# Turning the normed input of a gated-attention stage by DMA transposes through DRAM instead of TensorE transposes

## The chip, the cores and the metric

The kernel runs on one Trainium2 chip, on 8 cores. Every core runs the same program on its own stretch of 4096 tokens (plus 128 tokens of warm-up ahead of it), with its own copy of the weights; the cores exchange nothing. The time is that of the slowest core, in microseconds. The engines are called as in the profile: PE (TensorE, matrix products), PEld (its weight loads), DVE (VectorE), ACT (ScalarE), POOL (GpSimd) and SP (SyncE, which issues all DMAs here).

## The reference

One layer of gated linear attention, and one channel-mixing layer behind it, both in a residual frame with LayerNorms. The input is two sequences of 16384 tokens with 1024 features, in float32.

```python
def _L0_attn_ref(x, Wq, Wk, Wv, Wo, norm_w):
    q = silu(x @ Wq.T);  f = sigmoid(x @ Wk.T);  log_f = log_sigmoid(f)
    k = 1.0 - f;         v = x @ Wv.T
    out = _gla_scan(heads(q), heads(k), heads(v), heads(log_f))   # 8 heads of 128
    return _rmsnorm(out, norm_w) @ Wo.T
# _gla_scan, per token: S = exp(g) * S + k outer v ; o = q . S
def _L0_ffn_ref(x, W_r, W_k, W_v, mu_r, mu_k):
    xr = mu_r * x + (1 - mu_r) * x_prev;  xk = mu_k * x + (1 - mu_k) * x_prev
    return sigmoid(xr @ W_r.T) * (square(relu(xk @ W_k.T)) @ W_v.T)
x = x + layernorm(_L0_attn_ref(layernorm(x), ...))
x = x + layernorm(_L0_ffn_ref(layernorm(x), ...))
```

## The kernel before, in words

**Numbers in pairs.** Every float32 operand of a matrix product is held as two bf16 tensors, a high part (`_h`) and a low part (`_l`), and every product is three bf16 products added in PSUM: high by high, high by low, low by high.

**Tiles.** A tile `p` is 256 tokens (tile 0 has the 128 of warm-up alone), in two chunks `j` of 128. There are `nt` = 17 tiles, 0 to 16. Stage A computes q, k, v and the attention, and writes its output to the DRAM tensors `oh_scr` and `ol_scr`. Stage B reads it back, applies Wo and the first residual, and does the channel mixing with three more weights. Weights of stage B take the SBUF places of stage A's as these come free; between the stages lies a stretch in which both are interleaved by hand.

**One tile of stage A.** The tokens of tile p+1 are loaded as `xt` (128 tokens on the partitions, 2 chunks, 1024 features, float32). `ln_stats` finds mean and variance, `ln_apply` (line 394, ACT) norms `xt` in place. The matrix products need the features on the partitions, so `turn_x` transposes: for each chunk and each half of the features, four PE transposes of 128x128 in float32 into one PSUM bank (line 409), then ACT copies the bank to bf16 as `lnh` (line 416), and DVE subtracts that from the bank to give `lnl` (line 418). `lnh` and `lnl` each have two buffers, for even and odd tiles.

**The order of the work** is written out by hand. A helper appends each instruction to its engine's list, with semaphore waits; each engine runs its list in order. The loop over p = 2 to 15 issues, in this order: `k_tile(p)` (k of the tile, 192 products, line 251), `ln_stats(p+1)`, `gate(p)`, `gla_scores(p-1,0)` (lines 547 and 572, results split as `A_h`, `A_l`, `Ax_h`, `Ax_l`), `q_job(p,0)` and `(p,1)` (line 251), `ln_apply(p+1)`, `scan(p,0)` (line 481, DVE), `gla_out(p-1,0)` (line 607), `gla_scores(p-1,1)`, `q_job(p,2)` and `(p,3)`, `scan(p,1)`, `gla_rms(p-1,0)` (line 632), `gla_out(p-1,1)`, `turn_x(p+1)`, `load_x(p+2)`, `v_job(p,0,0)` (line 234), `gla_rms(p-1,1)`, `store_o(p-1)`, `prep(p,0)`, and the other three `v_job`s with `prep(p,1)`. Thus `turn_x` is called for tiles 3 to 16 in this loop, and for tiles 0 to 2 ahead of it. `k_tile(p+1)`, the first use of the turned tile, is the first thing PE does in the next round.

**PSUM** is a ring of 8 banks: `take()` hands out the next, and its user first waits until the bank's last reader is done. `turn_x` takes four of them for each tile.

**DMAs** are all on SP's list, in order, among them the load of `xt` (which waits until the last transpose has read the tile), and the stores of `os_h` and `os_l` to `oh_scr` and `ol_scr`. `wst` is a buffer of 8 KB on each partition in which the last two rows of blocks of each weight land; after the weights of stage A it is not used until stage B's come.

Of the kernel before, what the change touches and what calls it, by code (L numbers as in the profile page):

```python
# [9 lines left out]
ALU = mybir.AluOpType  # L10
# [82 lines left out]
def build_program(tok, warm):  # L93
# [16 lines left out]
    oh_scr = nc.dram_tensor("oh_scr", [nt * 128, NCH * TILE], BF16).ap()  # L110
    ol_scr = nc.dram_tensor("ol_scr", [nt * 128, NCH * TILE], BF16).ap()

    xNc = xN.rearrange("(n p) d -> p n d", p=128)
    outNc = outN.rearrange("(n p) d -> p n d", p=128)

    def o_dram(scr, p):
# [1 line left out]

    ctx = ExitStack()
    sets = {"wk": 0, "wq": 1, "wv": 2, "wo": 0, "wk2": 1, "wr": 2, "wv2": 0}  # L120
    bld = Bld(nc, ctx, ["LC", "LI", "LX", "LX0", "LX1", "LO0", "LO1", "SO", "SB0", "SB1",
                        "V", "S", "G", "T"] + [f"W{i}{ci}" for i in range(3) for ci in range(NCH)])
    op, ev, C = bld.op, bld.ev, bld.cnt

    def sb(stack, name, shape, dt):
        return stack.enter_context(nc.sbuf_tensor(name, shape, dt))
# [16 lines left out]
    aa = sb(ctx, "aa", [128, 6], F32)  # L143
    bb = sb(ctx, "bb", [128, 6], F32)
    rv = sb(ctx, "rv", [128, 2], F32)
    wst = sb(ctx, "wst", [128, 2, D], F32)
    ring = [ctx.enter_context(nc.psum_tensor(f"ps{i}", [128, 512], F32)) for i in range(8)]

# [184 lines left out]
    with ExitStack() as early:  # L333
        with ExitStack() as first:
# [13 lines left out]

    at = {"xt": [], "lnT": [[], []], "kf": [], "qs": [], "gb": [], "ebq": [], "ebk": [], "pl": [],
          "qt": [[], []], "kt": [[], []], "kx": [[], [], []], "vt": [[], [], []], "A": [],  # L350
          "Ax": [], "os": [], "osq": [], "rv": [[], []]}
    ck = {}

    def half_of(p):
# [45 lines left out]
    def turn_x(p, js=None, banks=None):  # L400
        for j in js or half_of(p):
            xj = x_of(p, j)
            dh, dl, js = ln_of(p, j)
            free = at["lnT"][p % 2] if p else []
            for g in range(2):
                i, bank = (banks[g], ring[banks[g]]) if banks else take()
                for b in range(4):
                    c = 4 * g + b
                    op("tensor", lambda e, b=b, c=c, xj=xj, bank=bank: e.transpose(  # L409
                        bank[:, b * 128:(b + 1) * 128], xj[:, c * 128:(c + 1) * 128],  # L410
                        ident[:]),
                       wait=[ln_ab[p, j], ev_id] + ring_free[i] if b == 0 else (),
                       inc=[("T", 1)] if b == 3 else ())
                evt = ev("T")
                b3 = bank[:].rearrange("p (c n) -> p c n", n=128)
                evh = sop(lambda e, g=g, js=js, dh=dh, b3=b3: e.activation(
                    out=dh[:, 4 * g:4 * g + 4, js], in_=b3, func=AF.Copy), evt, *free)
                evl = vop(lambda e, g=g, js=js, dh=dh, dl=dl, b3=b3: e.tensor_tensor(
                    dl[:, 4 * g:4 * g + 4, js], b3, dh[:, 4 * g:4 * g + 4, js],
                    ALU.subtract), evh)  # L420
                ring_free[i] = [evl]
        if p == 0:
            at["kf0"] = [evt]
        else:
            at["xt"] = [evt]
        ck[p] = dict(lnT=evl)

    def put_k(p, i, bank, evt, blocks):
        kp, _, _, fs = own(p)
# [44 lines left out]
    def v_job(p, j, half, *waits):  # L474
        xh, xl, js = ln_of(p, j)
        put_v(p, j, half, *tok_job(xh, xl, js, *pair("wv"), half, *waits))

    def scan(p, j):
        _, _, gp, js = own(p, j)
        for h in range(H):  # L480
            evb = op("vector", lambda e, h=h: e.tensor_tensor_scan(  # L481
                gp[:, h, js], gp[:, h, js], gp[:, h, js], 0.0, ALU.add, ALU.bypass),
                wait=[("V", C["V"]), ck[p]["g"]] if h == 0 else (), inc=[("V", 1)], nop=True)
        ck[p][f"b{j}"] = evb
# [103 lines left out]
    def gla_out(p, j):  # L588
        n = 2 * p - 1 + j
        js = slice(j * 128, (j + 1) * 128)  # L590
        c = ck[p]
        s0, s1 = n % 3, (n - 1) % 3
        for g4 in range(2):
            i, bank = take()
            parts = [(s0, ((vt_h, A_h), (vt_h, A_l), (vt_l, A_h)), [c[f"A{j}{g4}"], c[f"v{j}"]])]
            if n > 0:
                bp, bj = before(p, j)
                parts.append((s1, ((vt_h, Ax_h), (vt_h, Ax_l), (vt_l, Ax_h)),
                              [c[f"X{j}{g4}"], ck[bp][f"v{bj}"]]))
            for k, (sv, pairs, waits) in enumerate(parts):  # L600
                for m in range(12):
                    h = 4 * g4 + m // 3
                    vo, ao = pairs[m % 3]
                    cs = slice((m // 3) * 128, (m // 3 + 1) * 128)
                    first, last = k == 0 and m == 0, k == len(parts) - 1 and m == 11
                    op("tensor", lambda e, vo=vo, ao=ao, sv=sv, h=h, cs=cs, g4=g4, first=first,
                       last=last, bank=bank: e.matmul(  # L607
                           bank[:, cs], vo[:, sv, h, :], ao[:, g4, cs], start=first, stop=last),
                       wait=waits + (ring_free[i] if first else []) if m == 0 else (),
                       inc=[("T", 1)] if last else ())  # L610
            evt = ev("T")
            b3 = bank[:].rearrange("p (h n) -> p h n", n=128)
            h4 = slice(4 * g4, 4 * g4 + 4)
            evh = sop(lambda e, b3=b3, h4=h4: e.activation(
                out=os_h[:, h4, js], in_=b3, func=AF.Copy), evt, *at["os"])
            evq = sop(lambda e, g4=g4, bank=bank: e.activation(
                out=osq[:, g4 * 512:(g4 + 1) * 512], in_=bank[:], func=AF.Square), *at["osq"])
            evl = vop(lambda e, b3=b3, h4=h4: e.tensor_tensor(
                os_l[:, h4, js], b3, os_h[:, h4, js], ALU.subtract), evq)
            ring_free[i] = [evl]  # L620
        at["A"] = at["Ax"] = [evt]
        at["vt"][s1] = [evt]
        c[f"o{j}"] = evl
        c[f"sq{j}"] = evq
# [109 lines left out]
    for p in range(2, nt - 1):  # L734
        k_tile(p)
        ln_stats(p + 1)
        if p == 2:
            gla_out(0, 1)
        gate(p)
        gla_scores(p - 1, 0)  # L740
        if p == 2:
            gla_rms(0, 1)
            store_o(0)
        q_job(p, 0)
        q_job(p, 1)
        ln_apply(p + 1)
        scan(p, 0)
        gla_out(p - 1, 0)
        gla_scores(p - 1, 1)
        q_job(p, 2)  # L750
        q_job(p, 3)
        scan(p, 1)
        gla_rms(p - 1, 0)
        gla_out(p - 1, 1)
        turn_x(p + 1)
        if p + 2 < nt:
            load_x(p + 2)
        v_job(p, 0, 0)
        gla_rms(p - 1, 1)
        store_o(p - 1)  # L760
        prep(p, 0)
        v_job(p, 0, 1)
        v_job(p, 1, 0)
        prep(p, 1)
        v_job(p, 1, 1)
        bld.flush()
# [348 lines left out]
```

How the kernel before makes its waits and increments, by code:

```python
        def closure(e, fn=fn, waits=waits, incs=tuple(incs), nop=nop):  # L51
            for sem, v in waits:
                e.wait_ge(sem, v)
            if nop:
                e.engine_nop()
            ins = fn(e)
            for sem, k in incs:
                ins.then_inc(sem, k)
# [11 lines left out]
        def closure(e, waits=waits):  # L70
            for sem, v in waits:
                e.wait_ge(sem, v)
```

## Time and profile before

| what | value |
|---|---|
| time, median of 3 runs | 2744.53 us |
| the profiled execution's own time | 2742.91 us |
| its span (slowest core, core 2) | 2741.1 us |
| spans of all 8 cores | 2739.5 to 2741.1 us |
| PE busy | 2635.0 us (96%) |
| DVE busy | 1279.0 us (47%) |
| ACT busy | 1113.5 us (41%) |
| POOL busy | 409.6 us (15%) |
| DMA, mean over the span | 43 GB/s |
| mean granted clock of PE | 0.984 |

The span is the time between the first and the last instruction of a core, and lies 1.8 us under the execution's own time. Busy shares are averages over two stages and the stretch between them: the loop of stage A runs from about 150 to 1205 us, the stretch between to about 1430 us, and stage B from there to the end. The granted clock is 1.00 where the chip lets PE run at its upper level of 2.4 GHz throughout, and 0.50 where it is held at the lower, 1.2 GHz. A busy PE says that products are in its pipeline, so what an instruction costs there is read from the distance between starts, as the chain of waits and the timeline give it, and not from its duration.

### The profile page before, as it was taken

The numbers are of one execution on the slowest core, as the hardware profiler recorded it, in microseconds if no ns is written. First come the engines' busy times: TensorE is split into PE (matmuls) and PEld (weight loads), VectorE is DVE, ScalarE is ACT, GpSimd is POOL, SyncE is SP. The second block draws the span as 40 slices with busy tenths as digits, with TensorE's granted clock in tenths as the row PEclk, the third lists the DMA queues.
The fourth block names the chain that finished last, engine by engine and source line by source line (L and its number), as shares of the span: only waits on it lengthen the run. The fifth ranks groups of instructions, "written<-read, shape, count | busy, mean of one in ns | idle before, by whom it ended". The sixth has DMA issues, their size and how long they took to land.

```text
span 2741.1 us, 53464 instructions; the slowest of 8 cores (2739.5 to 2741.1 us)
## 1 busy us (share of the span) xinstructions
PE 2635.0 (96%) x19752; PEld 1783.9 (65%) x19752; DVE 1279.0 (47%) x2148; ACT 1113.5 (41%) x1349; POOL 409.6 (15%) x350
## 2 busy tenths in 40 slices
PE   6989999999999999998749999999999999999998
PEld 5778777777788877775436555665565654556544
DVE  6354444444444443435555444544445444454443
ACT  4555555555555555555343222222222222222222
POOL 0223333232222333322000000000000000000000
PEclk9999999999999999999879999999999999999999
DMA  7000010001000010024230011100111001110000
GB/s 226 17 10 31 32 32 32 32 32 32 32 33 29 5 32 32 32 62 139 78 108 22 34 39 47 46 33 24 39 47 47 32 24 39 47 47 32 24 27 28
DMA packets 39888, 118.97 MB, mean 43 GB/s; under 512 B 11728, under 2 KB 11984, under 8 KB 39632
## 3 DMA queue, kind: packets, MB, share of 16 engines
q1 hardware_dynamic: 39632, 115.56, 12.4%
q8 instruction: 160, 2.62, 0.4%
q14 instruction: 96, 0.79, 0.1%
HBM read 81.47 MB, written 34.08 MB: 42 GB/s over the span
## 4 chain that ended last, share of the span: by engine, by line
PE 88%; DVE 5%; ACT 3%; POOL 2%; issue 1%; DMA 1%; DVEq 0%; ACTq 0%; POOLq 0%; SPq 0%
PE ps L234 46%; PE ps L251 33%; PE ps L607 3%; PE ps L572 1%; PE ps L547 1%; PE ps L274 1%; PE ps L409 1%; PE ps L845 1%; DVE st L287 1%; DVE wk L213 1%; DMA wst<-wqT 1%; DVE gb L481 0%; POOL ebk L500 0%; DVE wr L213 0%; POOL kx_l L525 0%
## 5 line engine op out<-in xcount | busy, mean ns | idle before, releaser
L251 PE MATMUL ps<-xk_h,wk 128*128 128x256 bf16 x2048 | 340.4, 274 | 3.5 <-DVE wk L213 3.5
L251 PE MATMUL ps<-lnh,wq 128*128 128x256 bf16 x1920 | 322.1, 274 | 0.0
L234 PE MATMUL ps<-wo,o_h 128*128 128x512 bf16 x1056 | 314.7, 380 | 2.7 <-DVE A_l L558 2.7
L251 PE MATMUL ps<-lnh,wk 128*128 128x256 bf16 x1920 | 316.9, 273 | 0.0
L234 PE MATMUL ps<-wr,xr_h 128*128 128x512 bf16 x1024 | 306.5, 381 | 10.3 <-DVE wr L213 10.3
L234 PE MATMUL ps<-wv,lnh 128*128 128x512 bf16 x1056 | 314.1, 379 | 0.0
L234 PE MATMUL ps<-wv,kc_h 128*128 128x512 bf16 x1024 | 304.6, 379 | 0.0
L251 PE MATMUL ps<-xk_l,wk 128*128 128x256 bf16 x1024 | 280.3, 274 | 0.0
L251 PE MATMUL ps<-lnl,wq 128*128 128x256 bf16 x960 | 263.0, 274 | 0.0
L251 PE MATMUL ps<-lnl,wk 128*128 128x256 bf16 x960 | 261.7, 273 | 0.0
L292 POOL TENSOR_TENSOR aa<-v,mhalf 128x1 f32<-128x1 f32 x98 | 53.7, 548 | 1157.4 <-DVE v L290 1157.1
L251 PEld LDWEIGHTS ps<-xk_h,wk 128*128 128x128 bf16 x2048 | 201.3, 98 | 29.2 <-issue 3.6
L251 PEld LDWEIGHTS ps<-lnh,wq 128*128 128x128 bf16 x1920 | 188.8, 98 | 22.4
L251 PEld LDWEIGHTS ps<-lnh,wk 128*128 128x128 bf16 x1920 | 187.9, 98 | 23.2
L234 PE MATMUL ps<-wo,o_l 128*128 128x512 bf16 x528 | 200.4, 380 | 0.0
L234 PE MATMUL ps<-wv,lnl 128*128 128x512 bf16 x528 | 200.1, 379 | 0.0
L234 PE MATMUL ps<-wr,xr_l 128*128 128x512 bf16 x512 | 195.1, 381 | 0.0
L234 PE MATMUL ps<-wv,kc_l 128*128 128x512 bf16 x512 | 194.1, 379 | 0.0
L234 PEld LDWEIGHTS ps<-wr,xr_h 128*128 128x128 bf16 x1024 | 100.5, 98 | 132.3 <-issue 12.8
L234 PEld LDWEIGHTS ps<-wo,o_h 128*128 128x128 bf16 x1056 | 103.4, 98 | 124.2 <-issue 3.4
L234 PEld LDWEIGHTS ps<-wv,lnh 128*128 128x128 bf16 x1056 | 102.1, 98 | 117.5
L234 PEld LDWEIGHTS ps<-wv,kc_h 128*128 128x128 bf16 x1024 | 100.2, 98 | 117.5
(146 smaller groups left out, 4460.6 us busy)
## 6 DMA issues: line engine op xcount, KB each, us to landing
xt<-xN SPq DMA_DIRECT2D x16, 1024.0 KB, 8.1
x<-xN SPq DMA_DIRECT2D x16, 1024.0 KB, 5.7
outN<-x SPq DMA_DIRECT2D x32, 512.0 KB, 2.7
oh_scr<-os_h SPq DMA_DIRECT2D x16, 512.0 KB, 8.8
ol_scr<-os_l SPq DMA_DIRECT2D x16, 512.0 KB, 9.6
o_h<-oh_scr SPq DMA_DIRECT2D x15, 512.0 KB, 4.2
o_l<-ol_scr SPq DMA_DIRECT2D x15, 512.0 KB, 5.1
wk_f<-wkT SPq DMA_DIRECT2D x6, 512.0 KB, 11.8
```

Of the source, the lines that this page charges most:

```text
L213: evl = vop(lambda e, ci=ci, sl=sl: e.tensor_tensor(wl[:, ci, :], sl, wh[:, ci, :], ALU.subtract), evh)
L234: op("tensor", lambda e, xo=xo, wo=wo, ci=ci, first=first, last=last: e.matmul(bank[:], xo[:, ci, js], wo[:, ci, hs], start=first, stop=last),
L251: last=last: e.matmul(bank[:, os], wo[:, ci, ds], xo[:, ci, ts], start=first, stop=last),
L274: first=first, last=last: e.matmul(bank[:, cs], so(ci), mo(ci), start=first, stop=last),
L287: vop(lambda e, src=src, h=h: e.bn_stats(st6[:, k, 6 * h:6 * h + 6], src), *waits[h])
L292: evp = gop(lambda e: e.tensor_tensor(aa[:, k:k + 1], v1[:, k:k + 1], mhalf[:], ALU.pow), ev1, ev_set, *ab_free[k])
L409: op("tensor", lambda e, b=b, c=c, xj=xj, bank=bank: e.transpose(bank[:, b * 128:(b + 1) * 128], xj[:, c * 128:(c + 1) * 128], ident[:]), ...
L547: op("tensor", lambda e, ko=ko, qo=qo, h=h, cs=cs, m=m, bank=bank: e.matmul(bank[:, cs], ko[:, sl, h, :], qo[:, sl, h, :], start=m == 0, s ...
L572: op("tensor", lambda e, ko=ko, qo=qo, h=h, cs=cs, m=m, bank=bank: e.matmul(bank[:, cs], ko[:, sx, h, :], qo[:, sl, h, :], start=m == 0, s ...
L607: last=last, bank=bank: e.matmul(bank[:, cs], vo[:, sv, h, :], ao[:, g4, cs], start=first, stop=last),
L845: op("tensor", lambda e, b=b, c=c, bank=bank: e.transpose(bank[:, b * 128:(b + 1) * 128], lnd[:, j, c * 128:(c + 1) * 128], ident[:]), wai ...
```

## The change

Tiles 3 to 16 (the calls in the loop) no longer go through `turn_x`. In its place:

- `ln_pair(p+1)`, right behind `scan(p,0)`: for each chunk ACT copies the normed `xt` to bf16 and DVE subtracts the copy from `xt`, both 128x1024, still with the tokens on the partitions. The pair lies in a new buffer `lnp`, which has the SBUF place of `wst`.
- `turn_dma(p+1)`, behind `load_x(p+2)` on SP's list: one DMA writes `lnp` (1 MB) to a DRAM tensor `ln_scr`, and when it has landed, two DMA transposes (256x1024 in bf16, 512 KB each) read it back turned, into `lnh` and `lnl`.
- `load_x(p+2)` waits for the last subtraction of `ln_pair` instead of the last PE transpose.
- `k_tile(p+1)` waits for the second DMA transpose. The PSUM ring is asked for 26 banks in a round instead of 30.

```diff
+    ln_scr = nc.dram_tensor("ln_scr", [4 * TILE, D], BF16).ap()
...
+    with ExitStack() as raw:
+        lnp = sb(raw, "lnp", [128, 2, 2, D], BF16)
     wst = sb(ctx, "wst", [128, 2, D], F32)
...
+    def ln_pair(p):
+
+        for j in range(2):
+            evh = sop(lambda e, j=j: e.activation(out=lnp[:, 0, j, :], in_=xt[:, j, :],
+                                                  func=AF.Copy),
+                      ln_ab[p, j], *wst_free[0], *wst_free[1])
+            evl = vop(lambda e, j=j: e.tensor_tensor(lnp[:, 1, j, :], xt[:, j, :],
+                                                     lnp[:, 0, j, :], ALU.subtract), evh)
+        at["xt"] = [evl]
+
+    def turn_dma(p):
+
+        b = p % 2
+        rows = ln_scr[2 * b * TILE:(2 * b + 2) * TILE, :]
+        evs = dma(rows.rearrange("(a j p) d -> p (a j) d", a=2, p=128),
+                  lnp[:].rearrange("p a j d -> p (a j) d"), "SL", *at["xt"], *at["turned"][b])
+        wst_free[0] = wst_free[1] = [evs]
+        for a, dst in enumerate((lnh[b], lnl[b])):
+            evt = op("sync", lambda e, a=a, dst=dst: e.dma_start_transpose(
+                out=dst[:], in_=rows[a * TILE:(a + 1) * TILE, :]),
+                wait=[evs] + at["lnT"][b], inc=[("LT", 16)])
+        at["turned"][b] = [evt]
+        ck[p] = dict(lnT=evt)
...
         scan(p, 0)
+        ln_pair(p + 1)
         gla_out(p - 1, 0)
...
         gla_out(p - 1, 1)
-        turn_x(p + 1)
         if p + 2 < nt:
             load_x(p + 2)
+        turn_dma(p + 1)
         v_job(p, 0, 0)
```

The change moves line numbers by up to 30. On SP, one round of the loop before (the load of `xt`, the two stores of attention output):

```order
L159 DMA xt<-xN 128x2x1024
L159 DMA oh_scr<-os_h 128x2048
L159 DMA ol_scr<-os_l 128x2048
L87 UNCONDITIONAL_BRANCH
L159 DMA xt<-xN 128x2x1024
L159 DMA oh_scr<-os_h 128x2048
```

The same place on SP now:

```order
L163 DMA xt<-xN 128x2x1024
L163 DMA ln_scr<-lnp 128x4x1024
L451 DMA_TRANSPOSE lnh<-ln_scr 128x8x256
L451 DMA_TRANSPOSE lnl<-ln_scr 128x8x256
L163 DMA oh_scr<-os_h 128x2048
L163 DMA ol_scr<-os_l 128x2048
```

Three DMAs have come in between the load and the stores.

On ACT, from the norming of `xt` to the first `v_job`'s copy, before (`os_h` and `osq` are `gla_out`'s results, `vt_h` is v's high part):

```order
L394 ACTIVATE xt<-xt,bb,aa 128x1024 x2
L614 ACTIVATE os_h<-ps 128x4x128
L616 ACTIVATE osq<-ps 128x512
L614 ACTIVATE os_h<-ps 128x4x128
L616 ACTIVATE osq<-ps 128x512
L554 ACTIVATE A_h<-ps 128x512 x2
L578 ACTIVATE Ax_h<-ps 128x512 x2
...
L616 ACTIVATE osq<-ps 128x512
L416 ACTIVATE lnh<-ps 128x4x128 x4
L445 ACTIVATE vt_h<-ps 128x512
```

The same stretch of ACT now:

```order
L399 ACTIVATE xt<-xt,bb,aa 128x1024 x2
L436 ACTIVATE lnp<-xt 128x1024 x2
L643 ACTIVATE os_h<-ps 128x4x128
L645 ACTIVATE osq<-ps 128x512
L643 ACTIVATE os_h<-ps 128x4x128
L645 ACTIVATE osq<-ps 128x512
L583 ACTIVATE A_h<-ps 128x512 x2
L607 ACTIVATE Ax_h<-ps 128x512 x2
...
L645 ACTIVATE osq<-ps 128x512
L474 ACTIVATE vt_h<-ps 128x512
```

Four copies from PSUM behind `gla_out(p-1,1)` are gone, and two longer ones stand ahead of `gla_out(p-1,0)`'s results.

On DVE, around the scan of the first chunk (line 481 before), before, from the last of the eight scans on:

```order
L481 SCALAR_TENSOR_TENSOR gb<-gb 128x128
L618 TENSOR_TENSOR os_l<-ps,os_h 128x4x128 x2
L552 TENSOR_TENSOR ps<-ps,mask 128x512 x2
L558 TENSOR_TENSOR A_l<-ps,A_h 128x512 x2
L580 SCALAR_TENSOR_TENSOR Ax_l<-ps,Ax_h 128x512 x2
```

And now:

```order
L510 SCALAR_TENSOR_TENSOR gb<-gb 128x128
L439 TENSOR_TENSOR lnp<-xt,lnp 128x1024 x2
L647 TENSOR_TENSOR os_l<-ps,os_h 128x4x128 x2
L581 TENSOR_TENSOR ps<-ps,mask 128x512 x2
L587 TENSOR_TENSOR A_l<-ps,A_h 128x512 x2
L609 SCALAR_TENSOR_TENSOR Ax_l<-ps,Ax_h 128x512 x2
```

Two subtractions now stand ahead of the work on `gla_out(p-1,0)` and `gla_scores(p-1,1)`.

## Rows read from the trace of the kernel before

**Rows 1.** The page's first part: busy time by engine.

```profile
PE 2635.0 (96%) x19752; PEld 1783.9 (65%) x19752; DVE 1279.0 (47%) x2148; ACT 1113.5 (41%) x1349; POOL 409.6 (15%) x350
```

**Rows 2.** Chain of waits, 675.9 to 755 us: start, length, what.

```profile
675.85 20.96 PE ps L251 x192
...
725.99 2.70 PE ps L607 x48
728.69 1.75 PE ps L409 x16
730.44 5.18 PE ps L234 x24
...
751.36 3.71 PE ps L251 x34
```

**Rows 3.** Busy time by window, core 2; the columns head the group.

```profile
core 2: us, PE busy (x) PEld busy (x) DVE busy (x) ACT busy (x) POOL busy (x), PEclk, DMA share, GB/s
...
675.85:751.36 75.51, 75.51 (x706) 59.82 (x705) 32.52 (x57) 42.10 (x53) 21.48 (x16) 1.00 0.08 29
```

**Rows 4.** Line 409 in the loop, 150 to 1300 us.

```profile
L409 PE MATMUL ps<-ident,xt x224: 272/273/278, 199.9 to 1183.2; 128*128 128x128 f32 x112
```

**Rows 5.** For whom PE waited, 150 to 1300 us: total, times, longest.

```profile
PE ps L572 <- ACT kf L430: 4.3, 1, 4.3
PE ps L632 <- ACT osq L616: 3.4, 2, 3.1
```

**Rows 6.** Timeline of ACT, 706 to 737 us.

```profile
710.87 2.63 ACT L394 ACTIVATE xt<-xt,bb,aa 128x1024 f32<-128x1024 f32 x2
713.70 0.60 ACT L614 ACTIVATE os_h<-ps 128x512 bf16<-128x512 f32 x1 [0.20 <-ACT xt L394]
...
720.14 1.34 ACT L578 ACTIVATE Ax_h<-ps 128x512 bf16<-128x512 f32 x2
...
730.53 2.83 ACT L416 ACTIVATE lnh<-ps 128x512 bf16<-128x512 f32 x4
735.72 0.60 ACT L445 ACTIVATE vt_h<-ps 128x512 bf16<-128x512 f32 x1 [2.36 <-PE ps L234]
```

**Rows 7.** Timeline of DVE, 706 to 737 us.

```profile
707.23 2.84 DVE L481 TENSOR_TENSOR_SCAN gb<-gb 128x128 f32<-128x128 f32 x8 [0.20 <-DVE Ax_l L580]
715.14 0.69 DVE L618 TENSOR_TENSOR os_l<-ps,os_h 128x512 bf16<-128x512 f32 x1 [5.07 <-ACT osq L616]
...
722.02 0.69 DVE L580 SCALAR_TENSOR_TENSOR Ax_l<-ps,Ax_h 128x512 bf16<-128x512 f32 x1 [0.17 <-DVE Ax_l L580]
722.91 2.83 DVE L481 TENSOR_TENSOR_SCAN gb<-gb 128x128 f32<-128x128 f32 x8 [0.20 <-DVE Ax_l L580]
...
731.35 0.69 DVE L418 TENSOR_TENSOR lnl<-ps,lnh 128x512 bf16<-128x512 f32 x1 [0.17 <-DVE os_l L618]
```

**Rows 8.** Lines 502 and 504: durations in ns, minimum, median, maximum.

```profile
L502 ACT ACTIVATE qt_h<-ebq x33: 1057/1057/1058, 120.0 to 1282.0; 128x1024 bf16<-128x1024 f32 x33
...
L504 DVE TENSOR_TENSOR qt_l<-ebq,qt_h x33: 1225/1762/1989, 121.2 to 1283.2; 128x1024 bf16<-128x1024 f32 x33
```

**Rows 9.** Timeline of SP, 706 to 737 us: DMAs issued.

```profile
730.52 0.38 SPq L159 DMA_DIRECT2D xt<-xN  x1
731.25 0.32 SPq L159 DMA_DIRECT2D oh_scr<-os_h  x1
731.66 0.38 SPq L159 DMA_DIRECT2D ol_scr<-os_l  x1
```

**Rows 10.** DMA issues: count, KB each, us from issue to landing.

```profile
x<-xN SPq DMA_DIRECT2D x16, 1024.0 KB, 5.7
...
ol_scr<-os_l SPq DMA_DIRECT2D x16, 512.0 KB, 9.6
...
wv_f<-wvT SPq DMA_DIRECT2D x6, 512.0 KB, 18.3
...
o_h<-oh_scr SPq DMA_DIRECT2D x3, 256.0 KB, 6.7
...
oh_scr<-os_h SPq DMA_DIRECT2D x1, 256.0 KB, 3.1
```

**Rows 11.** Windows of 10 us, columns as in group 3.

```profile
150.00:160.00 10.00, 7.57 (x93) 6.91 (x91) 3.94 (x6) 4.07 (x6) 6.62 (x4) 1.00 0.01 2
160.00:170.00 10.00, 5.07 (x43) 4.25 (x44) 4.40 (x10) 8.30 (x11) 3.42 (x4) 0.51 0.00 1
170.00:180.00 10.00, 10.00 (x76) 8.24 (x75) 6.09 (x14) 6.93 (x8) 2.19 (x3) 0.81 0.27 55
```

More of the change, by code:

```diff
@@ L120, in build_program @@
     sets = {"wk": 0, "wq": 1, "wv": 2, "wo": 0, "wk2": 1, "wr": 2, "wv2": 0}
-    bld = Bld(nc, ctx, ["LC", "LI", "LX", "LX0", "LX1", "LO0", "LO1", "SO", "SB0", "SB1",
+    bld = Bld(nc, ctx, ["LC", "LI", "LX", "LX0", "LX1", "LO0", "LO1", "SO", "SL", "LT", "SB0", "SB1",
                         "V", "S", "G", "T"] + [f"W{i}{ci}" for i in range(3) for ci in range(NCH)])
@@ L350, in build_program @@
           "qt": [[], []], "kt": [[], []], "kx": [[], [], []], "vt": [[], [], []], "A": [],
-          "Ax": [], "os": [], "osq": [], "rv": [[], []]}
+          "Ax": [], "os": [], "osq": [], "rv": [[], []],
+          "turned": [[], []]}
     ck = {}
```

## The prediction

> **What bounds the kernel now.** I read the busy times first: PE is busy 96% of the span, no other engine half of it [rows 1]. That is an average, so next came the chain of waits through one round of stage A's loop [rows 2]. There the reader is to see that every piece from one `k_tile` (675.85 us) to the next (751.36 us) is PE's own, each starting where the last ended: PE is never released by anybody in these 75.51 us. The busy window says the same: 75.51 of 75.51 us, at a granted clock of 1.00, the upper level of 2.4 GHz, while DVE works 32.5 us, ACT 42.1 us and the DMA engines are 8% busy [rows 3]. In the whole loop PE waits for another engine three times, 7.7 us together, all near 160 us [rows 5, 11]. So in this stage a microsecond taken from PE is a microsecond off the time, as long as everything else stays inside the shorter round; and nothing taken from ACT or DVE is worth anything by itself.
>
> **What the change removes from PE.** The 16 transposes of a tile stand in the chain for 1.75 us, from 728.69 to 730.44 [rows 2], or 109 ns from start to start (the 273 ns of a single one is its way through the pipeline [rows 4]). Line 409 has 224 of them in the loop, at 199.9 to 1183.2 us, with no spread in their durations (272 to 278 ns), so 14 tiles at one price [rows 4]. 14 x 1.75 = **24.5 us**. The transposes of tiles 0 to 2 stay.
>
> **What it removes from ACT and DVE.** Four copies (2.83 us) and four subtractions of 0.69 us behind `gla_out(p-1,1)` [rows 6, 7]. Neither engine is waited for there: ACT idled 2.36 us before the copy of the first `v_job`, until PE had finished it [rows 6]. Worth nothing, but that copy and the `prep` chain behind it start 1.75 us earlier, as PE does, so the rear part of the round moves as a block.
>
> **What it adds to ACT and DVE, ahead of work that PE waits for.** A copy of 128x1024 to bf16 took 1.06 us and a subtraction of that shape 1.76 us (1.23 to 1.99) [rows 8]. ACT is done with norming at 713.50 us and was late already: `os_h` began 0.20 us behind it [rows 6]. Two copies with gaps put `os_h` 2.4 us later, at 716.1. On DVE the first subtraction starts when the first copy ends, about 714.9, the second ends near 718.6; DVE was idle for 5.07 us before 715.14 [rows 7], so the first hides. The subtraction for `os_l`, which started at 715.14, now starts at 718.8. Behind it stand the masks, `A_l` and `Ax_l` of `gla_scores(p-1,1)`. Their last ended at 722.71 [rows 7]; DVE loses its small gaps, ACT's `A_h` and `Ax_h` (from 720.14) move too [rows 6], and I work the last out to end near 725.5, 2.8 us later. Who waits for it: `gla_out(p-1,1)` on PE, at 725.99 [rows 2], under cover of the two `q_job`s. It needs the first `Ax_l` only behind 12 of its 48 products, and the second later still. The cover is eaten but holds: **0 us**. If it didn't hold, each microsecond late costs one per tile, 14 us in all. The second scan ends near 728.6 instead of 725.7: only `prep` reads it, which stands behind the copy of the first `v_job` (735.72 before [rows 6]). The ring: with 26 banks per round each job takes a bank used by another job 8 places earlier; the closest case is the first `v_job`, whose bank then comes from `gla_scores(p-1,1)`, free near 724 and wanted at 728.7. The 56 takes left out are seven turns of the ring, so stage B has the banks it had.
>
> **What it adds on SP and the DMA engines.** This decides the case. Data are ready at 718.6 us. SP first issues the load of `xt` (now at about 718.8 instead of 730.52), then the store of 1 MB. Before, a load of 1 MB and stores of 1 MB went out from 730.52 to 731.66 and the last landed 9.6 us behind its issue, so 2 MB took 10.7 us from first issue to last landing [rows 9, 10]. The same 2 MB now: landed by 729.5. SP stands in its wait until then. Queued behind it are the transposes and then the two stores of attention output, whose data are not ready before about 730 anyway, and whose next reader in line, the overwriting of `os_h`, comes a round later, at 713.70 plus a round [rows 6]. `k_tile(p+1)` wants the turned pair at 751.36 - 1.75 = 749.6. So the two DMA transposes, 1 MB in all, have **20.1 us**; every microsecond over that stalls PE by one in each of 14 rounds, and PE has nothing else in its list to do.
>
> No DMA transpose is in this trace, so its time D for the pair has to be bounded. Fast end: a plain load of 1 MB with nothing in its way, 5.7 us [rows 10]: 14 us to spare. Middle: pieces of 256 bytes. The first store of `os_h` goes in such pieces (128 tokens in bf16), 256 KB in 3.1 us, four of which are 12.4 us: hidden. The read of `oh_scr` in like pieces took 6.7 us for 256 KB, in other traffic, which gives 26.8 us: 6.7 us late [rows 10]. Slow end: a 512 KB load that stood in a full queue took 18.3 us, twice that is 36.6 us: 16.5 us late [rows 10]. I take the store of 256-byte pieces, 12.4 us, since the queue is nearly empty here (29 GB/s in a round [rows 3]), and so a cost of 0.
>
> The Trainium skill, page "Advanced Engine Details and Errata", section "X-Bar Transpose (TRN2)", says that transposing DMAs on this chip are as fast as plain ones, at 350 to 400 GB/s; by it the pair would take an estimated 3 us and the sum is the same. No row here shows it.
>
> **The sum.** Span 2741.1 - 24.5 = 2716.6; the execution's own time 2742.9 - 24.5 = 2718.4; the median of the runs lies 1.6 us over that execution, so **2720.0 us**, 0.9% faster. A measurement of this kernel can tell about 2% from no change, so this counts as within 2%.
>
> **Rival 1: the transposes are late, somewhat.** Place: PE in front of `k_tile(p+1)`, releaser the second transpose. Point from which it decides: D over 20.1 us; from 21.9 us on the kernel is slower than before, from 25.8 us by over 2% (55 us / 14 = 3.9 us per tile, and the 1.75 given back). With 26.8 us: 14 x (6.7 - 1.75) = +69 us, 2814 us. It can be worse: where PE idled 7.4 us between 150 and 170 us, the clock stood at 0.51 and then 0.81 for 10 us each, a loss of 10 x (0.49 + 0.19) = 6.8 us [rows 11]. If each stall does that, 14 x 11.75 = +165 us, 2909 us. For it speaks that 256-byte pieces have been that slow once; against it, that this was in a stretch with much other traffic.
>
> **Rival 2: the transposes go block by block and are far too slow.** At 36.6 us: 14 x (16.5 - 1.75) = +207 us, 2951 us, and 3047 us with the loss of clock. The extreme is a transpose that moves single elements: 262,144 for each of two parts at 3.1 us per 1024 pieces [rows 10] are 1.6 ms per tile and some 22 ms in all.
>
> The Trainium skill, page "VectorE: DVE Perf Modes", section "The three transpose paths", puts 1309 ns on one 128x128 block through the DMA path; the pair has 32 blocks, and by an estimate from that page, if they go one behind another, 42 us, 22 us late, about 3025 us. This is the rule that speaks against the change; no row here shows whether blocks overlap.
>
> **Rival 3: ACT and DVE run out of cover.** `A_l` and `Ax_l` come 1 to 2 us behind PE's need instead of 0.5 us ahead, because DVE's subtractions take their slow form and ACT falls behind. It gives back 14 to 28 us: 2734 to 2748 us. The work lies 2.8 us closer to PE than before, which speaks for it; the order of the products in `gla_out`, which asks for `Ax_l` last, against.
>
> That the change doesn't do what it says is out: the program's order has the 14 groups of transposes gone from PE.
>
> **Chances.** Forecast 0.70 (2714 to 2734 us); rival 3 0.05; rival 1 0.07; rival 2 0.17; anything that makes it faster by over 2%, 0.01. The most likely is 2720. The range must leave out no more than 2 in 10: it goes from 2712 to 2909, which has the forecast, rival 3 and rival 1 with its clock loss (0.82), and leaves rival 2 out. A part of rival 1 (D between 20.1 and 25.8 us) is still within 2%: same 0.77, slower 0.22, faster 0.01.
>
> **What would show it.** Right: in a round of the loop the chain holds PE alone and `k_tile` starts are 73.76 us apart; line 409 has 40 transposes left; the two DMA transposes land before about 750 us minus what earlier rounds saved; PE has no wait on them; `Ax_l` ends just before `gla_out`. Wrong: a wait of PE in front of `k_tile` with a DMA into `lnl` as its releaser, rounds of over 75.5 us, and a granted clock under 1.00 in them. What would make the forecast wrong is above all D, and next the landing of the store, since the store and the transposes share the same 30.8 us.

## Result and the profile after

The time of the changed kernel, in the executions that are compared, is 2719.8 us against 2744.5 us: a ratio of 0.991, 95% interval 0.9894 to 0.9927. That is 24.7 us less, on a forecast of 24.5 us. The profiled execution took 2719.81 us, with spans of 2716.4 to 2718.0 us. (Some executions of either kernel ran with one die or both at a lower granted clock and are left out of every comparison here, so a median over all of them would mislead.) A second series later gave 2718.5 to 2719.8 us for the same kernel (median 2719.3), beside 2743.1 us for the kernel before: 23.8 us less.

The busy times of the page, for the slowest core (core 0), beside [rows 1]:

```profile
PE 2601.8 (96%) x19383; PEld 1758.8 (65%) x19528; DVE 1274.3 (47%) x2120; ACT 1109.7 (41%) x1321; POOL 409.5 (15%) x350
```

The chain of waits through one round of stage A's loop, beside [rows 2] (start, length, what; where the record of a product is missing, the chain is interrupted by 0.05 us of "issue"):

```profile
664.79 20.96 PE ps L255 x192
...
714.93 2.70 PE ps L636 x48
717.63 0.05 issue
717.68 5.13 PE ps L238 x23
...
738.55 20.96 PE ps L255 x192
```

From one `k_tile` to the next are 738.55 - 664.79 = 73.76 us, where it was 75.51. The piece of 1.75 us between `gla_out` and the first `v_job` is gone, and nothing has come in its place. The window (core 0; columns as in [rows 3]) says that PE runs through, at a granted clock of 1.00, with more than twice the DMA share:

```profile
664.79:738.55 73.76, 73.60 (x688) 58.06 (x689) 32.21 (x55) 41.83 (x51) 21.48 (x16) 1.00 0.22 58
```

For whom PE waited between 150 and 1250 us, beside [rows 5]: the same two entries, and no DMA. (Up to 1300 us there is a third, 9.8 us for `lnd` near 1280, in the stretch between the stages. The kernel before has it too, with 9.4 us, behind 1300.)

```profile
PE ps L601 <- ACT kf L459: 4.3, 1, 4.3
PE ps L661 <- ACT osq L645: 3.4, 2, 3.1
```

What goes on meanwhile is on SP. Its timeline through the same round (start, time that SP needs to issue, what):

```profile
706.72 0.38 SPq L163 DMA_DIRECT2D xt<-xN  x1
707.25 0.39 SPq L163 DMA_DIRECT2D ln_scr<-lnp  x1
718.08 2.72 SPq L451 DMA_TRANSPOSE lnh<-ln_scr  x1
720.95 2.37 SPq L451 DMA_TRANSPOSE lnl<-ln_scr  x1
723.41 0.74 SPq L163 DMA_DIRECT2D oh_scr<-os_h  x1
724.25 0.38 SPq L163 DMA_DIRECT2D ol_scr<-os_l  x1
```

and from the list of DMA issues, the time from issue to landing in us:

```profile
ln_scr<-lnp SPq DMA_DIRECT2D x14, 1024.0 KB, 10.7
...
lnh<-ln_scr SPq DMA_TRANSPOSE x14, 5.8
lnl<-ln_scr SPq DMA_TRANSPOSE x14, 5.6
```

The store is issued at 707.25 and the first transpose at 718.08, when it has landed. By the median of the list, the second transpose lands 5.6 us behind 720.95, at about 726.6: the pair has taken D = 8.5 us, and `k_tile` wants it at 738.55. So 11.9 us are left over.

On DVE the timeline shows what [rows 7] showed, with the two subtractions in front:

```profile
704.02 1.23 DVE L439 TENSOR_TENSOR lnp<-xt,lnp 128x1024 bf16<-128x1024 f32 x1 [5.00 <-ACT lnp L436]
705.42 1.23 DVE L439 TENSOR_TENSOR lnp<-xt,lnp 128x1024 bf16<-128x1024 f32 x1 [0.17 <-DVE lnp L439]
706.82 0.69 DVE L647 TENSOR_TENSOR os_l<-ps,os_h 128x512 bf16<-128x512 f32 x1 [0.17 <-ACT osq L645]
...
713.64 0.69 DVE L609 SCALAR_TENSOR_TENSOR Ax_l<-ps,Ax_h 128x512 bf16<-128x512 f32 x1 [0.17 <-DVE Ax_l L609]
```

The last `Ax_l` ends at 714.33, 0.6 us before `gla_out` begins at 714.93. Before it was 722.71 against 725.99, 3.3 us [rows 2, 7]. The cover proper is larger, since `gla_out` asks for the first `Ax_l` only at its 13th product: that product starts at 715.46 by PE's timeline, and the first `Ax_l` ended at 713.47, 2.0 us earlier.

### The profile page after: what moved, and what is told of

The parts are those of the page before. It is cut to its first block, busy times and chain, and to the rows that moved or that the text cites. A ratio compares the mean times of both kernels' runs of the same rounds, so it can differ in the third digit from the quotient of the medians.

```text
span 2718.0 us, 52729 instructions; the slowest of 8 cores (2716.4 to 2718.0 us)
## 1 busy us (share of the span) xinstructions
PE 2601.8 (96%) x19383; PEld 1758.8 (65%) x19528; DVE 1274.3 (47%) x2120; ACT 1109.7 (41%) x1321; POOL 409.5 (15%) x350
## 2 busy tenths in 40 slices
DMA packets 105517, 148.30 MB, mean 55 GB/s; under 512 B 70192, under 2 KB 70448, under 8 KB 105264
## 4 chain that ended last, share of the span: by engine, by line
PE 86%; DVE 5%; ACT 3%; issue 2%; POOL 2%; DMA 1%; DVEq 0%; ACTq 0%; POOLq 0%; SPq 0%
PE ps L238 45%; PE ps L255 33%; PE ps L636 3%; PE ps L576 1%; PE ps L601 1%; PE ps L278 1%; PE ps L875 1%; DVE st L291 1%; DMA wst<-wqT 1%; DVE xm L897 1%; DVE wk L217 1%; POOL ebk L529 0%; DVE wr L217 0%; DVE gb L510 0%; DVE x L854 0%
## 5 line engine op out<-in xcount | busy, mean ns | idle before, releaser
L238 PE MATMUL ps<-wr,xr_h 128*128 128x512 bf16 x994 | 300.2, 381 | 11.2 <-DVE wr L217 10.3
L238 PE MATMUL ps<-wv,lnh 128*128 128x512 bf16 x1023 | 307.0, 379 | 2.5
L238 PE MATMUL ps<-wo,o_l 128*128 128x512 bf16 x513 | 194.8, 380 | 0.1
L238 PE MATMUL ps<-wv,lnl 128*128 128x512 bf16 x513 | 194.5, 379 | 0.1
L238 PE MATMUL ps<-wv,kc_l 128*128 128x512 bf16 x497 | 188.5, 379 | 0.1
## 6 DMA issues: line engine op xcount, KB each, us to landing
ln_scr<-lnp SPq DMA_DIRECT2D x14, 1024.0 KB, 10.7
```

The costliest lines, as they stand in the source:

```text
L238: op("tensor", lambda e, xo=xo, wo=wo, ci=ci, first=first, last=last: e.matmul(bank[:], xo[:, ci, js], wo[:, ci, hs], start=first, stop=last),
```

## Experiments

The theory to test has three parts: the gain is PE's 1.75 us per tile and nothing else; the DMA route is free as long as store and transposes fit in their room; and ACT and DVE sit inside PE's need by little. The rivals: part of the gain or of the cost lies on ACT and DVE, or in the traffic. All line numbers are those of the kernel in question.

### Nothing turned at all (e1_no_turn)

```diff
-        ln_pair(p + 1)
...
+        ck[p + 1] = dict(lnT=ln_ab[p + 1, 1])
+        at["xt"] = [ln_ab[p + 1, 1]]
         if p + 2 < nt:
             load_x(p + 2)
-        turn_dma(p + 1)
```

> Leaves out the turning of tiles 3 to 16 altogether: no copy to bf16, no subtraction, no store, no transposes; k, q and v of these tiles are worked out from what stood in the buffers. My theory: the new route costs nothing, so this takes what the changed kernel takes, 2720 us (within 2 us). Rival: the new route costs something that only a comparison shows (contention, cover eaten on ACT and DVE); then this is faster than the changed kernel by 14 times that cost, 2706 us for 1 us per tile.

Measured: 2720.1 to 2720.8 us, ratio to the kernel before 0.9918 (0.9898 to 0.9937). Without copies, subtractions, stores and transposes the kernel is no faster than with them (2718.5 to 2719.8 us). So the new route costs nothing that can be measured, and taking the turning away altogether wins no more than this change does.

### PE turns as before, the pair is made and stored besides (e2_both)

```diff
+        pair_ev = list(at["xt"])
+        turn_x(p + 1)
+        at["xt"] = at["xt"] + pair_ev
         if p + 2 < nt:
             load_x(p + 2)
-        turn_dma(p + 1)
+        store_pair(p + 1, pair_ev)      # the store of turn_dma alone
```

> PE still turns tiles 3 to 16 as in the kernel before, and the bf16 pair is made and stored to DRAM besides (no DMA transposes, nobody reads the pair). My theory: the whole gain is the 1.75 us of PE per tile, and what was added is free, so this takes what the kernel before takes, 2744.5 us (within 2 us). Rival: part of the gain came from relieving ACT and DVE behind the transposes; here they carry both loads, and it would be slower than before, by 14 us for each microsecond that PE is kept waiting in a round.

Measured: 2744.2 to 2745.1 us, ratio 1.0013 (1.0000 to 1.0026). ACT and DVE carry the old load and the new, and the time is that of the kernel before beside it (median 2743.2) to 1.7 us. With PE's transposes back the gain is gone, so the gain is PE's. The chain of waits has the transposes back at their old price:

```profile
727.65 2.70 PE ps L644 x48
730.36 1.75 PE ps L414 x16
732.11 5.18 PE ps L238 x24
```

### The transposes two, three and four times (e3_twice, e4_thrice, e4b_four)

The pair of transposes is issued again when the last one has landed, so that only D grows:

```diff
-        for a, dst in enumerate((lnh[b], lnl[b])):
-            evt = op("sync", ..., wait=[evs] + at["lnT"][b], inc=[("LT", 16)])
+        for _ in range(2):          # 3, 4
+            gate_ev = [evs] + at["lnT"][b] + ([evt] if _ else [])
+            for a, dst in enumerate((lnh[b], lnl[b])):
+                evt = op("sync", ..., wait=gate_ev, inc=[("LT", 16)])
```

> The pair of DMA transposes is done twice, the second time when the first has landed. In the trace of the changed kernel the store lands 53.3 us behind the start of k_tile, the pair takes about 8.5 us more, and the next k_tile starts at 73.76 us: 11.9 us to spare. A second pair uses 8.5 of them. My theory: still hidden, 2720 us. Rival (traffic of the transposes slows something that PE reads or waits for): slower by 14 us for each microsecond per tile.

> The pair of DMA transposes is done three times, one behind the other: 25.5 us instead of 8.5, against 20.4 us of room, so 5.1 us late per tile. My theory: PE waits in front of k_tile in 14 rounds, 2720 + 14 x 5.1 = 2791 us if a stall of that length costs only itself. Rival: each such stall also lowers the granted clock, as the 7.4 us near 160 us seem to do, and costs up to 6.8 us more: up to 2887 us, with a granted clock under 1.00 behind each stall.

> The pair of DMA transposes is done four times, one behind the other. With three, a pair took about 8.0 us there and PE waited 1.7 us per tile. My theory: a fourth pair makes the transposes the bound, so each further microsecond is paid in full: 1.7 + 8.0 = 9.7 us of waiting per tile, 2720 + 14 x 9.7 = 2856 us, plus the clock: stalls of this length lower the granted clock in the k_tile behind them and cost 3 to 7 us more each, 2898 to 2954 us in all. Rival: the clock doesn't matter at this length, 2856 us.

| pairs of transposes | us | ratio to before (95%) | PE waits for `lnl` in the loop |
|---|---|---|---|
| 1 (the change) | 2719.8 | 0.991 (0.9894 to 0.9927) | none |
| 2 | 2718.8 to 2719.9 | 0.9914 (0.9895 to 0.9933) | none |
| 3 | 2745.2 to 2753.7 | 1.0027 (1.0013 to 1.0041) | 18.3 us in 11 rounds (core 1) |
| 4 | 2873.6 to 2900.5 | 1.0449 (1.0354 to 1.0544) | 118.0 us in 14 rounds (core 0), 110.9 (core 2) |

With two pairs, SP's timeline shows both landed before `k_tile` at 738.76:

```profile
717.75 2.45 SPq L453 DMA_TRANSPOSE lnh<-ln_scr  x1
720.35 2.81 SPq L453 DMA_TRANSPOSE lnl<-ln_scr  x1
725.73 1.78 SPq L453 DMA_TRANSPOSE lnh<-ln_scr  x1
727.71 3.69 SPq L453 DMA_TRANSPOSE lnl<-ln_scr  x1
```

The second pair starts 8.0 us behind the first, and its end is near 733.1 (5.4 us, the median to landing, behind the last issue): 5.6 us left over. Doubling everything the DMA transposes do costs nothing, so twice their traffic is still free.

With three pairs the wait that the prediction's first rival described appears, in its place and with its releaser. It is 1.7 us in the mean of the 11 rounds that have one, 1.3 per tile, and not the 5.1 I had expected. A repeated pair took about 8.0 us instead of 8.5 (1.0 us for two of them), and the store landed in 8.7 us (median) instead of 10.7, which makes 3.0 of the 3.8 us; the rest isn't accounted for. The waits of PE on core 1 (total, times, longest) and two windows over a `k_tile`, the one behind the longest wait (3.95 us), the other behind one of 1.36 us:

```profile
PE ps L255 <- DMA lnl<-ln_scr: 18.3, 11, 4.0
```

```profile
681.00:705.00 24.00, 23.21 (x188) 19.76 (x189) 6.37 (x12) 6.53 (x8) 8.76 (x6) 0.86 0.10 41
759.00:781.00 22.00, 21.13 (x196) 18.98 (x197) 7.61 (x14) 8.69 (x11) 9.59 (x6) 1.00 0.12 46
```

And the same two in the chain of waits, with what released the second:

```profile
681.78 23.93 PE ps L255 x192
...
753.86 5.76 DMA lnl<-ln_scr
759.63 0.25 issue
759.87 21.12 PE ps L255 x192
```

(Behind a wait the chain counts a piece 0.16 us longer than the distance between starts; from first product to next line's first product, by PE's timeline, these two are 23.76 and 20.96 us.) Behind the wait of 4.0 us the granted clock was 0.86 and `k_tile` took 2.8 us more than its 20.96; behind the short wait the clock was 1.00 and it took no more. In the same run, the waits of 2.83 and 2.19 us were followed by a `k_tile` of 22.50 and 22.63 us at a clock of 0.92, one of 2.48 us by 20.95 at 1.00, and all of 0.3 to 1.7 us by 20.95 or 20.96 at 1.00. So the short waits cost themselves alone here, and of the four longer ones three brought a loss of clock, of 1.5 to 2.8 us each. The sum closes: 18.3 us waited and 6.0 us of clock are 24.3 of the 26 us by which core 1 is longer than the cores of the change.

With four pairs PE waits in every round, up to 10.8 us on core 2, the slowest:

```profile
PE ps L255 <- DMA lnl<-ln_scr: 110.9, 14, 10.8
```

110.9 / 14 = 7.9 us of waiting per tile. But core 2 is a poor one to read the clock from. It and core 3 show a granted clock of about 0.8 from 150 to 327 us, also between the stalls, and its first round with a stall took 94.2 us, 16.2 more than the round and its wait. Core 0 doesn't have that. Its span is 2865.1 us, 147 over the 2718 of the change, or 10.5 us per tile: 118.0 / 14 = 8.4 waited, and 2.1 lost otherwise. The `k_tile`s behind the first 13 of its waits, of 6.7 to 12.1 us, took 22.3 to 23.7 us, so 2.0 more than 20.96 in the mean, at clocks of 0.87 to 0.94. So the loss of clock per stall did not grow with the stall: the wait of 4.0 us with three pairs had cost 2.8. I had expected 9.7 us of waiting and 3 to 7 of clock (2898 to 2954 us). Both were overrated, the wait as with three pairs, and the fastest execution, 2873.6 us, lies between the two theories, nearer to the one with the clock left out (2856 us).

### Plain loads instead of transposes (e6_plain)

```diff
-            evt = op("sync", lambda e, a=a, dst=dst: e.dma_start_transpose(
-                out=dst[:], in_=rows[a * TILE:(a + 1) * TILE, :]), ...)
+            evt = op("sync", lambda e, a=a, dst=dst, src_p=src_p: e.dma_start(
+                out=dst[:].rearrange("p (j c) n -> p j (c n)", j=2), in_=src_p), ...)
```

> The two DMA transposes are replaced by two plain loads of the same 512 KB each from the same rows of DRAM into the same tiles, in rows of 2 KB, untransposed: the products of tiles 3 to 16 get unturned input. Theory that a transpose is as fast as a plain DMA: a load lands in the 5.6 to 5.8 us of the transposes, and the issue takes SP as long. Theory that the 256-byte pieces set the pace: the plain loads land in 3 to 4 us, and SP is done with an issue in 0.4 us instead of 2.4 us. Either way the time is 2720 us, since all of it is under cover.

This version ran once. Six of the eight cores had spans of 2715.0 to 2718.0 us, the same as the change; two stood at 2722 us with a granted clock of 0.977, which made its time 2724.14 us. SP's timeline on one of the two (core 1) and the landings:

```profile
705.95 0.37 SPq L163 DMA_DIRECT2D ln_scr<-lnp  x1
715.02 0.36 SPq L452 DMA_DIRECT2D lnh<-ln_scr  x1
715.53 0.70 SPq L452 DMA_DIRECT2D lnl<-ln_scr  x1
```

```profile
lnh<-ln_scr SPq DMA_DIRECT2D x14, 512.0 KB, 4.9
lnl<-ln_scr SPq DMA_DIRECT2D x14, 512.0 KB, 6.1
```

The pair of plain loads is done at 715.53 + 6.1 = 721.6, in 6.6 us, where the transposes took 8.5. Neither theory had it quite: a plain load lands 4.9 or 6.1 us behind its issue, a transpose 5.8 or 5.6. What differs is when the second one goes out. It is issued 0.5 us behind the first with plain loads, and 2.9 us behind it with transposes (718.08 and 720.95), because SP needs 0.4 to 0.7 us to issue a plain load and 2.4 us in the median for a transpose. Those 2.4 us more at the second issue account for the 1.9 us between the pairs. The long issue also holds up what stands behind on SP's list.

### The copy and the subtraction two and three times (e5_pair2, e5_pair3)

```diff
+            for _ in range(2):          # 3
                 evh = sop(... lnp[:, 0, j, :] <- xt ...)
+            for _ in range(2):          # 3
                 evl = vop(... lnp[:, 1, j, :] <- xt - lnp[:, 0, j, :] ...)
```

> The copy and the subtraction that make the bf16 pair are each done twice: 2.3 us more on ACT and 2.8 us more on DVE, ahead of gla_out and gla_scores. In the trace of the changed kernel the last Ax_l ends at 714.33 us, 0.6 us ahead of gla_out(p-1,1) at 714.93. My theory (ACT and DVE are in line for PE here, and the cover is nearly used up): following the instructions through, the first Ax_l ends 1.4 us behind PE's need, so 14 x 1.4 = 20 us slower than the changed kernel, 2740 us. Rival (the cover is much larger than I worked out, since PE takes these results late): 2720 us.

> The copy and the subtraction are each done three times: 4.5 us more on ACT, 5.6 us more on DVE. My theory: PE waits 5.2 us per tile in gla_out(p-1,1) for Ax_l, 14 x 5.2 = 73 us, 2793 us, and more where the clock falls behind the stall. The rival of large cover: 2720 to 2740 us. The pair is ready about 8 us later for the store, which alone would still be under cover (11 us to spare).

With two, the fastest execution took 2737.6 us (20 expected over the change, 18 measured); the ratio to the kernel before isn't clear (0.9986, 0.9946 to 1.0027). On core 7, with a clock of 0.985 and a span of 2735.8 us, PE waits 14 times where the change had no wait at all:

```profile
PE ps L638 <- DVE Ax_l L611: 12.6, 14, 0.9
...
PE ps L638 <- DVE A_l L589: 1.1, 2, 0.7
```

The chain of waits shows the place, behind the first 12 of the 48 products:

```profile
724.16 0.70 DVE Ax_l L611
724.86 0.14 issue
725.00 2.17 PE ps L638 x36
```

This run also measures the cover: DVE had 2 x 1.40 = 2.8 us more to do, the start of one subtraction to that of the next being 1.40 us, and PE waited 0.9 us of them. So about 1.9 us were cover, as the 2.0 us read from the timeline above say, and not 0.6.

With three, 2838.2 us was the lowest (ratio to the kernel before 1.0286, 1.0235 to 1.0337), and 2811 us the span of cores 4 to 7 (clock 0.970). There PE waited, on core 4:

```profile
PE ps L638 <- DVE A_l L589: 46.2, 14, 3.6
PE ps L663 <- DVE os_l L649: 9.8, 14, 1.3
...
PE ps L638 <- DVE Ax_l L611: 4.2, 14, 0.4
```

60.2 us, 4.3 per tile, of the 5.2 expected; the other 34 of the 94 us over the change go with a granted clock of 0.96 between 150 and 1200 us, where the change has 1.00, and this number is less sure than the others. The rival of a large cover has fallen: one more copy and subtraction per chunk, on engines that are busy 41% and 47%, cost about 18 of the 24.7 us. Both were repeated together, so the runs don't say how much each of the two engines would cost alone.

### The same route in stage B too (e7_stage_b, e9_halves)

Stage B transposes its second normed input, `lnd`, on PE as well, 16 per tile (line 845 before, 875 after). Here it is split, stored and turned in pieces of 128 tokens, and DVE adds the two turned parts (shortened: a comment behind a `def` stands for its body):

```diff
+    def pair2(j):       # ACT: lnp[:, 0, j] <- lnd[:, j]; low2(j), DVE: the subtraction
+    def turn2(q, j):
+        evs = dma(rows[:, j]..., lnp[:, :, j, :], "SM", bt["pair"][j], ...)
+        for a in range(2):
+            evt = op("sync", ... e.dma_start_transpose(
+                out=xT[:, a, :, j * 128:(j + 1) * 128], in_=rows[a, j]), ...)
+    def join2(q, j):    # DVE: ln2T[:, :, 1 + 128 j ...] <- xT[:, 0] + xT[:, 1]
...
             wo_chunk(q + 1, 0)
-            wo_chunk(q + 1, 1)
+            pair2(0)
+            wo_chunk(q + 1, 1, lambda: low2(0))
+            pair2(1)
+            low2(1)
+            turn2(q + 1, 0)
+            turn2(q + 1, 1)
...
-            turn_chunk(0)
-            turn_chunk(1)
+            for j in range(2):
+                join2(q + 1, j) if q > 1 else turn_chunk(j)
```

> The same route in stage B as well: from the fourth tile on, the second normed input (lnd) is split token-major into a bf16 pair, stored to DRAM and turned by DMA transposes, 128 tokens at a time; DVE adds the two turned parts into ln2T, where before PE transposed and ACT copied. 14 more tiles lose 1.75 us of PE. My theory: in the trace of the changed kernel lnd is ready 14 us before its sum is wanted by diff, and diff has 5.7 us of room ahead of wk2_tile, of which 1.75 go with the shorter round; copy and subtraction 2.4 us, store of 512 KB 3 us, two transposes of 256 KB each 5 us, addition 1.2 us make 12 us, so all is hidden: 2720 - 24.5 = 2695.5 us, 1.8% under the kernel before. Rival: the route is longer than its cover here (the SP list is shared with the stores of the output), and PE waits in front of wk2_tile: slower than 2720 us from 1.75 us per tile on.

> The changed kernel itself once more, on the same chip as the version above, to compare the two directly: 2720 us.

Measured: 2703.3 to 2710.9 us, ratio to the kernel before 0.9853 (0.9817 to 0.9889); the changed kernel beside it 2718.5 to 2719.8 us, 0.9898 (0.9845 to 0.9952). The version beats both kernels, but lies 8 to 15 us over the 2695.5 expected. What PE waited for `xk_l` from 1400 us on, core 0 (span 2705.7 us), and below the same on core 4 (2693.9 us):

```profile
PE ps L256 <- DVE xk_l L939: 12.5, 9, 2.2
```

```profile
PE ps L256 <- DVE xk_l L939: 1.7, 2, 1.5
```

So the rival was half right: in some rounds the route doesn't fit into its cover, by up to 2.2 us on core 0 and 2.7 on core 5, and more often on some cores than on others. On SP's timeline this is the second half of the tokens (store, two transposes of 256 KB, which land in 3.8 us in the median; DVE could start on this half only at 1945.86, 6.3 us behind 1939.51):

```profile
1936.65 0.37 SPq L164 DMA_DIRECT2D ln_scr<-lnp  x1
1939.51 2.80 SPq L894 DMA_TRANSPOSE xT<-ln_scr  x2
```

Then the subtraction `diff` was cut in two, the first half to be done while the second half of the tokens is on its way:

```diff
+    def diff_half(j):
+        vop(lambda e: e.tensor_tensor(dmix[:, :, o], ln2T[:, :, n], ln2T[:, :, o],
+                                      ALU.subtract), *bt["T_ev"], *bt["T_mm"])
...
+            for j in range(2):
+                if q > 1:
+                    join2(q + 1, j)
+                    diff_half(j)
```

> As the version that turns both stages' inputs by DMA, but diff is done in two halves of 128 tokens, the first while the second half of the tokens is still on its way: 1.15 us less behind the last landing. In that version PE waited for xk_l in front of wk2_tile, 12.5 us in 9 tiles on core 0 (up to 2.2 us) and 1.7 us on core 4. Theory (the last landing is what ends late): about 9 us off the slowest core, 2697 us. Rival (what is late is DVE's own work behind it, whatever the landing): no change from 2706 us.

Measured: 2694.9, 2695.8 and 2699.5 us in the three executions that are compared, ratio 0.9832 (0.9812 to 0.9852), with spans of 2690.2 to 2694.0 us in the profiled one. PE's waits from 1400 us on have no `xk_l` left, on any core; on core 6 they are:

```profile
PE ps L239 <- DVE wr L218: 9.9, 1, 9.9
```

So the rival (no change) has fallen. The work from the last addition to the first `xk_l` is 1.1 us shorter (8.8 us before, 7.7 now). That alone doesn't cover waits of 2.2 us, and the timelines show a second part: the store of the second half goes out 24.2 us (median, core 1) ahead of the first product of `wk2_tile`, where it was 22.2 us ahead of the moment at which PE was ready for it (median, core 0). Why it goes out earlier was not tested. It is still close: in one round on core 1 `xk_l` is ready just in time. Both stages by DMA are 1.7% under the kernel before.

## Why the prediction was right

**PE is the bound, and 14 x 1.75 us is the gain.** Right: 24.7 us measured against 24.5, the round 73.76 us to the hundredth, and 40 transposes left on the line that had them. On core 2, `k_tile`'s first product starts at 133.8 us in both kernels, and its last one at 1225.1 and 1200.4 us, 24.7 less. The experiments that leave everything out and that keep both routes show that no other part of the change gives or takes more than 2 us. That the time agreed to 0.2 us is luck all the same. The start of the loop scatters by more (core 0: 132.7 and 135.1 us), the second series has 23.8 us, and the 1.6 us that the sum adds for the median of the runs over the profiled one were not there: 2719.76 and 2719.81 us. The slowest core's span was 2718.0 us, 1.4 over the 2716.6 of the sum, and that made up for it.

**ACT and DVE: cost 0, cover nearly used up.** Right in the cost. I had worked the end of the last `Ax_l` out at 725.5, 49.65 us behind the start of `k_tile`; it was 714.33 - 664.79 = 49.54. That agreement is luck, two errors of size cancelled. The subtraction took 1.23 us instead of the 1.76 taken from [rows 8], so `os_l` began 42.0 us behind `k_tile` instead of 42.95. And from there to the last `Ax_l` DVE took 7.5 us instead of 6.7, since the gap of 0.80 us in front of the second `os_l`, where it waits for ACT's `osq`, stayed. The size of the cover was wrong, in the safe direction. The 0.5 us of the prediction end where `gla_out` begins, but the text itself says that the first `Ax_l` is asked for only behind 12 of its 48 products, and left this out of the figure. The cover was 2.0 us, and one more copy and subtraction per chunk broke it (rival 3's mechanism, with waits of 0.9 us and a cost of 1.3 us per tile).

**The store.** Right: landed 53.3 us behind the start of `k_tile`, forecast 53.65, from the three issues of [rows 9]. Here too two errors cancelled: the load went out 1.0 us earlier than worked out (706.72 - 664.79 = 41.9, against 42.95), and load and store took 11.4 us from the first issue instead of 10.7.

**The transposes.** Right in sign, off in size: 12.4 us taken from the store in 256-byte pieces [rows 10], 8.5 measured. The number of pieces fits: the page counts 105517 packets against 39888 before, 4688 more per tile, and 1 MB in pieces of 256 bytes would be 4096 of them, the rows of the store 512. What was wrong is the multiplication. Four times the 3.1 us of one DMA of 256 KB counts the time from issue to landing four times over, one behind another, while here the second transpose was issued 2.9 us behind the first and before that had landed (5.8 us), so the two overlap. How much of the 8.5 us is pieces and how much is issue and way wasn't tested apart. The term fed a cover, so its error cost nothing.

The page "Advanced Engine Details and Errata" of the Trainium skill ("X-Bar Transpose (TRN2)": as fast as plain DMAs, 350 to 400 GB/s) isn't borne out in size here: counted from first issue to last landing, 1 MB in 8.5 us is 123 GB/s, against 159 GB/s for the same bytes by plain loads (6.6 us). The page "VectorE: DVE Perf Modes" of the Trainium skill ("The three transpose paths": 1309 ns for a block of 128x128 in bf16) would have given 42 us by an estimate for blocks one behind another; measured were 8.5 us / 32 = 0.27 us per block, so they don't go one behind another at that price, and rival 2 is out.

**The rivals' prices.** Rival 1's point of 20.1 us of room for D was about right: by the trace the room was 738.55 - 718.08 = 20.5 us, about 16 us (two pairs) cost nothing, and about 24 us (three) cost 1.3 us of waiting per tile, less than the 3.5 us over the room, as the store landed earlier there. Its uncertain part, the clock, came out between the two figures: 0 to 2.8 us per stall with three pairs, 2.0 in the mean with four (core 0), where the prediction's upper figure was 6.8. That figure counted the lower clock of 160 to 170 us over all 10 us, though PE was busy for only 5.07 of them. By the same rows, 5.07 x 0.49 + 10 x 0.19 is an estimate of 4.4 us.

**What I had not counted:** each transpose occupies SP for 2.4 us. It did no harm, as the stores behind it had slack; in a list where something urgent stands behind, it would have been a term of the sum.

## What to carry to other kernels

Where one engine is busy without a gap, work moved off it is worth exactly its distance from start to start, times the count, until the new route's latency reaches the next use; so add up issue, landing and wait from the moment the data are ready, and compare that with the start of the next use, before looking at bandwidth. Engines at 40 to 50% busy can still be in line for the bound one: follow the instructions behind the added ones through to the very product that reads them, and write down the cover that is left. When a transfer just misses its cover, cut the work behind its last landing in pieces before giving up the route. And when two figures agree to a tenth, look at the terms, since errors can cancel.

## What the runs showed of the hardware

- A DMA transpose of 256x1024 in bf16 took SP 1.9 to 4.2 us to issue (median 2.3 to 2.5), where a plain DMA of the same bytes took 0.4 to 0.7; it landed in 5.6 to 5.8 us in the median, the pair in 8.5 us. Where the pair was repeated (e4_thrice), the next one started 6.9 to 9.8 us behind it, 8.1 in the median. One of 128x1024 landed in 3.8 us (median, e7_stage_b; 3.0 to 6.3).
- After waits of 0.3 to 1.7 us PE's granted clock stayed at 1.00 (e4_thrice, core 1). After one of 4.0 us it was 0.86 over the next 24 us, which cost 2.8 us more. Waits of 2.19, 2.48 and 2.83 us cost 1.7, 0 and 1.5 us more. With waits of 6.7 to 12.1 us in every round (e4b_four, core 0) the clock behind them was 0.87 to 0.94 over the next 21 us, and the loss 1.3 to 2.7 us each.
- The subtraction of 128x1024 on DVE took 1.23 us here, and POOL's timeline is empty from 700 to 712 us. The case of 1.76 us in [rows 8] stood beside POOL's work at 742 and 755 us. That POOL is the cause was not tested.
